# Mamba block with a 16-expert MoE: the opening in another order, router logits by four column groups

## The reference, cut to what matters

```python
# mamba
xz = xn @ W_in;  x_in, z = split(xz)               # 512 channels each
u = silu(conv4(x_in) + conv_b)                     # causal, one filter per channel
dt, B, C = split(u @ W_xproj)                      # 16, 16, 16
delta = softplus(dt @ W_dt + b_dt)
h[t] = exp(delta*A) * h[t-1] + delta*u*B           # 512 channels x 16 states
y = (sum_n h*C + D_skip*u) * silu(z);  out = y @ W_out
# moe
w, idx = top2(softmax(xn @ Wr + br))               # 16 experts, weights renormalised
h = gelu(layernorm(xn @ W1[e] + b1[e]) * g1[e] + be1[e])
moe = sum over the two experts of w * (h @ W2[e] + b2[e])
```

## Time and profile before

| | us |
|---|---|
| median of 3 runs (lowest to highest) | 1169.85 (1165.87 to 1171.04) |
| the profiled execution | 1167.6 |
| its span, first to last instruction | 1165.8 |
| VectorE busy | 1050.6 (90%) |
| TensorE / ScalarE / GpSimd busy | 956.4 / 865.6 / 842.7 |
| VectorE idle before the router chain | 10.64 |

### The profile page before, as it was taken

One profiled execution on the slowest core, in us unless ns is written; L12 is line 12 of the kernel. 1 busy time (PEld: TensorE's weight loads), 2 busy tenths in 40 slices (PEclk: granted clock), 3 DMA queues, 4 the chain that ended last, 5 costly groups with the idle time before them and its releaser, 6 DMA issues.

```text
span 1165.8 us, 16719 instructions
## 1 busy us (share of the span) xinstructions
PE 956.4 (82%) x4498; PEld 642.5 (55%) x4499; DVE 1050.6 (90%) x1308; ACT 865.6 (74%) x1793; POOL 842.7 (72%) x550
## 2 busy tenths in 40 slices
PE   5955576696978989789887998799988999978775
PEld 2433244463556656566555766476556655656554
DVE  7599969999999899989688969999898989979994
ACT  3444597655789788777799689968998699867971
POOL 8005588888668677558677786977977767867994
PEclk9975897589889999799998999899998999789978
DMA  9987865764366523834437542763447452864413
GB/s 313 405 360 231 269 197 149 250 229 106 94 220 199 120 65 95 303 103 99 104 117 258 154 102 68 266 202 62 107 140 240 130 123 58 258 195 89 107 19 64
DMA packets 130295, 194.38 MB, mean 167 GB/s; under 512 B 20892, under 2 KB 113224, under 8 KB 121944
## 3 DMA queue, kind: packets, MB, share of 16 engines
q1 hardware_dynamic: 104944, 153.06, 39.4%
q0 software_dynamic: 18816, 23.14, 12.1%
q10 hardware_dynamic: 6440, 17.10, 4.0%
HBM read 146.34 MB, written 51.05 MB: 169 GB/s over the span
## 4 chain that ended last, share of the span: by engine, by line
PE 38%; ACT 17%; issue 16%; DVE 14%; POOL 8%; DMA 6%; ACTq 2%; SPq 0%; DVEq 0%; POOLq 0%
DVE hb L1463 9%; PE psY L1020 7%; PE psA L1045 6%; POOL hc L624 5%; ACT hb L785 4%; PE psC L1157 4%; PE psC L1107 3%; PE psA L1092 3%; PE psE L1134 2%; DVE psB L1452 2%; DMA xg<-meta 2%; ACT hnT L872 2%; PE psA L1037 2%; PE psA L1080 1%; ACT L875 1%
## 5 line engine op out<-in xcount | busy, mean ns | idle before, releaser
L624 POOL TENSOR_TENSOR hc<-hb,Cb 128x1024 f32<-128x1024 f32 x235 | 595.6, 2599 | 128.7 <-PE psY L1020 69.6
L1463 DVE TENSOR_TENSOR_SCAN hb<-hb,carry,psB 128x512 f32<-128x512 f32 x384 | 471.3, 1263 | 0.8 <-ACT hb L785 0.7
L1020 PE MATMUL psY<-ident,hc 128*128 128x128 f32 x2048 | 311.7, 293 | 66.3 <-POOL hc L624 52.4
L1020 PEld LDWEIGHTS psY<-ident,hc 128*128 128x128 f32 x2048 | 261.2, 152 | 186.2 <-issue 82.8
L785 ACT ACTIVATE hb<-delta,aneg 128x512 f32<-128x512 f32 x512 | 349.2, 717 | 15.4 <-DVE delta L1301 7.0
L1452 DVE TENSOR_TENSOR psB<-Bb,psU 128x512 f32<-128x512 f32 x512 | 325.1, 679 | 0.0
L664 POOL DMA_INDIRECT out<-yo,idx x80 | 127.9, 1599 | 66.1 <-ACT yo L885 21.3
L1463 DVE TENSOR_TENSOR_SCAN hb<-hb,psB 128x512 f32<-128x512 f32 x128 | 149.2, 1201 | 4.2 <-ACT hb L785 4.2
L1045 PE MATMUL psA<-ux,dgw 128*128 128x512 f32 x232 | 119.7, 626 | 11.8 <-ACT ux L729 11.7
L638 POOL DMA_INDIRECT xs_d<-xg,slots x64 | 68.4, 1068 | 47.5 <-issue 27.1
L1157 PE MATMUL psC<-w2r,hnT 128*128 128x256 f32 x320 | 89.7, 429 | 0.0
(11 more groups left out here) (211 smaller groups left out, 1199.2 us busy)
## 6 DMA issues: line engine op xcount, KB each, us to landing
Bb<-bc_d SPq DMA_DIRECT2D x32, 1024.0 KB, 6.4
Cb<-bc_d SPq DMA_DIRECT2D x32, 1024.0 KB, 7.1
w2r<-in_L_ffn_W SPq DMA_DIRECT2D x90, 256.0 KB, 3.2
w1r<-w1c_d SPq DMA_DIRECT2D x80, 256.0 KB
xs_d<-xg ACTq DMA_DIRECT2D x1, 10320.0 KB, 41.0
xg<-xs_d SPq DMA_DIRECT2D x20, 516.0 KB, 5.2
xg<-xn_d SPq DMA_DIRECT2D x64, 128.0 KB, 2.3
Bb<-in_L_attn_x SPq DMA_DIRECT2D x8, 512.0 KB, 9.0
```

Of the source, the lines that this page charges most:

```text
L624: pool.tensor_tensor(hc[:, k:k + 2, :], hb[:, g % HR:g % HR + 2, :], Cb[:, n:n + 2, :], ALU.mult).then_inc(s_g, 1)
L1020: mm = pe.matmul(y[:, tt * P:(tt + 1) * P], hc[:, g % GR, tt * P:(tt + 1) * P], ident[:, :], start=False, stop=(n == NS - 1), is_transpose ...
L1463: dve.tensor_tensor_scan(h, h, psB[g % 2][:, :], first, ALU.mult, ALU.add).then_inc(s_scan, 1)
```

## The change

- **Router logits.** The router weights get 32 columns (16 used, the rest zero), and each group's product is four matmuls of 128 tokens per half of the inputs, written to four bands of 32 PSUM partitions. One 128x128 eviction and one 128x128 transpose follow. Logits are copied out in two halves.
- **Constants.** GpSimd writes the identity, does group 0's root, then writes the other constants, waits for W_in and conv_w, and does the diagonal matrices after groups 1 to 4. The big zero memset of VectorE moves behind the first statistics. SyncE waits for two small memsets before it loads the router weights, and loads the bias four times.
- **First projection.** Quarters 0 and 1 are projected and convolved between router groups (rounds 2 to 7), 2 and 3 after them; quarters 0 to 2 take turns in psA. The rank matmuls stand between the convolutions of quarters 2 and 3.
- **Expert table.** Its four vector instructions move from the router chain to unit 40 of chunk 0.
- **Silu.** In every chunk the last tile of z, and the last quarter of x, goes from PSUM straight through silu, after the silu of the other three; the slots of `z_silu` move from 29 to 28, from 29 to 25 in chunk 0, from 31 to 30 in the last.

The diff, cut to its core and with indentation reduced:

```diff
-X0_FROM = 4
+ETAB_AT = 40
...
-    "x_copy": [13, 25, 34, 39],
+    "x_copy": [13, 25, 34],
...
-    "z_copy": [15, 17, 26, 28],
-    "z_silu": [29],
+    "z_copy": [15, 17, 26],
+    "z_silu": [28],
...
-    "z_copy": [14, 14, 24, 25],
-    "z_silu": [29],
+    "z_copy": [14, 14, 24],
+    "z_silu": [25],
...
-    "z_copy": [13, 20, 28, 30],
-    "z_silu": [31],
+    "z_copy": [13, 20, 28],
+    "z_silu": [30],
...
-wr = sb("wr", [P, KC, E])
+wr = sb("wr", [P, KC, 2 * E])
...
-brc = sb("brc", [E, 1])
+brc = sb("brc", [P, 1])
...
-lgT = [hc[0:E, k, :] for k in range(2)]
+lgT = [hc[:, k, 0:P] for k in range(2)]
...
-    return (psA, psC, psY[0], psY[1])[dc]
+    return (psA, psA, psA, psC)[dc]
...
+        if g == 0 and h == 0:
+            sp.wait_ge(s_etab, 1)
...
-    sp.dma_start(wr[:, :, :], Wr.rearrange("(k p) e -> p k e", p=P)).then_inc(s_w["early"], 16)
-    sp.dma_start(brc[:, :], br.rearrange("(e a) -> e a", a=1)).then_inc(s_w["early"], 16)
+    sp.wait_ge(s_cdve, 2)
+    sp.dma_start(wr[:, :, 0:E], Wr.rearrange("(k p) e -> p k e", p=P)).then_inc(s_w["early"], 16)
+    for k in range(TT):
+        sp.dma_start(brc[2 * E * k:2 * E * k + E, :], br.rearrange("(e a) -> e a", a=1)).then_inc(s_w["early"], 16)
...
-    sp.wait_ge(s_cdve, 1)
...
+    pool.wait_ge(s_const, 1)
     pool.affine_select(out=ident[:, :], in_=ident[:, :], compare_op=ALU.not_equal, fill=1.0,
                        base=0, pattern=[[-1, P]], channel_multiplier=1).then_inc(s_const, 1)
...
+    def constants():
+        pool.memset(upper[:, :], 0.0).then_inc(s_const, 1)
+        pool.memset(pick6[:, :, :], 1.0).then_inc(s_const, 1)
+        pool.memset(reset, 1.0).then_inc(s_const, 1)
+        pool.wait_ge(s_const, 5)
...
+        pool.iota(iotaM[:, :], pattern=[[1, MT]], base=0, channel_multiplier=0, **kw).then_inc(s_const, 1)
...
-    pool.wait_ge(s_cdve, NCONST)
+    pool.wait_ge(s_cdve, 3)
...
-        if g == 2:
+        if g == 0:
+            constants()
             pool.wait_ge(s_w["conv"], 32)
-            pool.wait_ge(s_const, 5)
-        if 2 <= g < 2 + DC:
-            conv_weights(g - 2)
+        if 1 <= g <= DC:
+            conv_weights(g - 1)
...
-    def x_silu(p):
-        act.wait_ge(s_xe, (p + 1) * DC)
+    def x_silu(p, bank):
...
+        act.wait_ge(s_xe, (p + 1) * DC - 1)
...
+        wrap = min(first + DC - 1, UR)
+        act.activation(ux[:, first:wrap, HALO:], ux[:, first:wrap, HALO:], ACT.Silu).then_inc(s_u, 1)
+        if wrap < first + DC - 1:
+            k = first + DC - 1 - UR
+            act.activation(ux[:, 0:k, HALO:], ux[:, 0:k, HALO:], ACT.Silu).then_inc(s_u, 1)
+        act.wait_ge(s_xp, (p + 1) * DC)
+        act.activation(u_of(p, DC - 1), bank[:, :], ACT.Silu, bias=col(cb, DC - 1)).then_inc(s_xe, 1)
         act.preload_act_table_set(LNEXP)
...
     def z_silu(c):
-        act.wait_ge(s_zc, (c + 1) * TT)
-        act.activation(zs[:, :, :], zs[:, :, :], ACT.Silu).then_inc(s_z, 1)
+        act.wait_ge(s_zc, (c + 1) * TT - 1)
+        act.activation(zs[:, 0:TT - 1, :], zs[:, 0:TT - 1, :], ACT.Silu).then_inc(s_z, 1)
+        z_free(c, TT - 1)
+        act.activation(zs[:, TT - 1, :], psA[:, :], ACT.Silu).then_inc(s_zc, 1)
         act.preload_act_table_set(LNEXP)
...
+    def logits(h):
+        act.wait_ge(s_lv, (h + 1) * NC // 2)
+        half = TILES // 2
+        act.activation(lg[:, h * half * E:(h + 1) * half * E].rearrange("p (i e) -> p i e", e=E),
+                       psE[:, :].rearrange("p (i w) -> p i w", w=2 * E)[:, :, 0:E], ACT.Copy).then_inc(s_lg, 1)
...
+        if g == NC // 2 + 2:
+            logits(0)
...
-            act.activation(lgT[(g - 1) % 2], (psC, psU)[(g - 1) % 2][0:E, :], ACT.Identity, bias=brc[:, :]).then_inc(s_lc, 1)
+            act.activation(lgT[(g - 1) % 2], (psC, psU)[(g - 1) % 2][:, 0:P], ACT.Identity, bias=brc[:, :]).then_inc(s_lc, 1)
...
-        if g == X0_FROM + 2:
-            x_in(0, 0, bank0(0))
+        if g in (3, 6):
+            x_in(0, g // 3 - 1, psA)
+        if g == 5:
+            x_copy(0, 0)
...
-    act.wait_ge(s_lv, NC)
-    act.activation(lg, psE[:, :], ACT.Copy).then_inc(s_lg, 1)
-    for dc in range(1, DC):
+    x_copy(0, 1)
+    logits(1)
+    for dc in range(2, DC):
...
-    act.wait_ge(s_vec, 1)
-    for dc in range(DC):
-        act.wait_ge(s_xp, dc + 1)
-        act.activation(u_of(0, dc), bank0(dc)[:, :], ACT.Silu, bias=col(cb, dc)).then_inc(s_xe, 1)
-    act.preload_act_table_set(LNEXP)
+    x_copy(0, 2)
+    x_silu(0, bank0(DC - 1))
...
-            pe.wait_ge(s_u, p)
+            pe.wait_ge(s_u, silus(p))
+            pe.wait_ge(s_xe, (p + 1) * DC)
...
-        pe.wait_ge(s_xe, dc + 1)
         if dc == 0:
-            pe.wait_ge(s_lg, 1)
+            pe.wait_ge(s_lg, 2)
+        elif dc == DC - 1:
+            pe.wait_ge(s_xe, DC)
...
-    pe.wait_ge(s_const, 15)
-    pe.wait_ge(s_cdve, NCONST)
-    pe.wait_ge(s_w["early"], 32)
+    pe.wait_ge(s_const, 2)
...
+            if g == 1:
+                pe.wait_ge(s_w["early"], 16 * (1 + TT))
...
             for kc in range(KC):
-                mm = pe.matmul((psC, psU)[(g - 1) % 2][0:E, :], wr[:, kc, :], xnTg[g - 1][:, kc, :],
-                               start=(kc == 0), stop=(kc == KC - 1))
+                for tt in range(TT):
+                    mm = pe.matmul((psC, psU)[(g - 1) % 2][2 * E * tt:2 * E * (tt + 1), 0:P], wr[:, kc, :],
+                                   xnTg[g - 1][:, kc, tt * P:(tt + 1) * P], start=(kc == 0), stop=(kc == KC - 1))
             mm.then_inc(s_lm, 1)
         if g >= 2:
             pe.wait_ge(s_lc, g - 1)
-            for tt in range(TT):
-                i = (g - 2) * TT + tt
-                mm = pe.matmul(psE[:, i * E:(i + 1) * E], lgT[g % 2][:, tt * P:(tt + 1) * P], ident[0:E, 0:E],
-                               start=True, stop=True, is_transpose=True)
-            mm.then_inc(s_lv, 1)
...
-        if g == X0_FROM:
-            pe.wait_ge(s_w["conv"], 32)
-            pe.wait_ge(s_vec, 1)
-        if X0_FROM <= g < X0_FROM + KC:
-            project(0, 0, g - X0_FROM, bank0(0))
-        elif g == NC - 1:
-            pe.wait_ge(s_wc, DC * KW)
-            for k in range(KW):
-                convolve(0, 0, k, bank0(0))
-    pe.wait_ge(s_te, 2 * NC)
-    for dc in range(1, DC):
-        if dc == 1:
-            pe.wait_ge(s_lc, NC)
+            if g == NC // 2 + 2:
+                pe.wait_ge(s_lg, 1)
+            i = (g - 2) % (NC // 2)
+            pe.matmul(psE[:, i * P:(i + 1) * P], lgT[g % 2], ident[:, :],
+                      start=True, stop=True, is_transpose=True).then_inc(s_lv, 1)
+        if g in (2, 5):
+            if g == 2:
+                pe.wait_ge(s_w["conv"], 32)
+                pe.wait_ge(s_vec, 1)
+            else:
+                pe.wait_ge(s_xe, 1)
+            for kc in range(KC):
+                project(0, g // 3, kc, psA)
+        elif g in (3, 4, 6, 7):
+            dc = (g - 3) // 3
+            pe.wait_ge(s_wc, (dc + 1) * KW)
+            for k in range(KW // 2):
+                convolve(0, dc, g % 3 * 2 + k, psA)
...
+    pe.wait_ge(s_lc, NC)
+    for dc in range(2, DC):
+        if dc == 2:
+            pe.wait_ge(s_xe, 2)
         for kc in range(KC):
             project(0, dc, kc, bank0(dc))
-    for dc in range(1, DC):
+    pe.wait_ge(s_wc, DC * KW)
+    for dc in range(2, DC):
         for k in range(KW):
             convolve(0, dc, k, bank0(dc))
-    pe.wait_ge(s_w["big"], 16 * NBIG)
-    for dc in range(DC):
-        if dc == 0:
+        if dc == 2:
+            pe.wait_ge(s_const, 15)
+            pe.wait_ge(s_cdve, NCONST)
+            pe.wait_ge(s_te, 2 * NC)
             pe.wait_ge(s_rtd, 2)
             pe.matmul(psB[0][:, :], upper[:, :], Mb, start=True, stop=True).then_inc(s_rank, 1)
             pe.matmul(psB[1][:, :], onesb[:, :], Mb, start=True, stop=True).then_inc(s_rank, 1)
+    pe.wait_ge(s_w["big"], 16 * NBIG)
+    pe.wait_ge(s_u, silus(0))
+    for dc in range(DC):
...
-    dve.memset(zero, 0.0).then_inc(s_cdve, 1)
+    dve.memset(wr[:, :, :], 0.0).then_inc(s_cdve, 1)
+    dve.memset(brc[:, :], 0.0).then_inc(s_cdve, 1)
+    dve.memset(mhalf[:, :], -0.5).then_inc(s_cdve, 1)
...
     row_stats(0)
+    dve.memset(zero, 0.0).then_inc(s_cdve, 1)
     row_norm(0)
...
-    over = zs[:, 0:3, :].rearrange("p a b -> p (a b)")
-    cmp_t = over[:, 0:MT * E].rearrange("p (j e) -> p j e", e=E)
-    link(dve.tensor_tensor(cmp_t, s16(9).unsqueeze(1).to_broadcast([P, MT, E]),
-                           iotaT.rearrange("p (j e) -> p j e", e=E), ALU.is_le))
-    tf = over[:, MT * E:MT * E + MT]
-    link(dve.tensor_reduce(tf, cmp_t, AX.X, ALU.add))
-    link(dve.tensor_scalar(tf, tf, float(E - 1), None, ALU.min))
-    link(dve.tensor_copy(etab[:, :], tf))
+    link(dve.tensor_copy(tiles_to[:, :], s16(9)))
     dve.memset(small[:, 0, 0:1], 0.0).then_inc(s_route, 1)
     d_max(0, 0)
+    def tile_experts():
+        room = yo[:, :, :].rearrange("p a b -> p (a b)")
```

(30 more changed lines are left out.)

51 lines of the change are left out of this document (24 added, 27 removed).

## The result

The changed kernel took 1176.41 us (median of 8 runs; 1173.92 to 1186.44), the kernel before 1169.24 in runs on the same chip: ratio 1.0072, 95% interval 1.0042 to 1.0102. (One of the 8 runs of the kernel before took 1283.49 us, far above all others, and is not in the ratio.) It is **slower by 0.7%**; forecast was 1160.6 and faster, with a range up to 1176. The profiled execution took 1173.99 us (span 1172.3) against 1167.6.

What follows compares the result with a forecast made beforehand. VectorE, busy 90% of the span, was taken as the bound. Savings of 2.0 (router chain), 3.0 (chunk 0) and 4.2 us (other chunks) sum to -9.2: 1158.4 profiled, 1160.6 as median, range near 1149 to near 1176.

Steps and rivals of the forecast that it cites:

- Part 1: The start, up to router group 2: TensorE begins it at 19.6 in place of 19.46 us, +0.1.
- Part 2: TensorE from group 2 to the logits: terms sum to +1.2 us, logits at about 49.1.
- four abreast: Rival, router products: four bands run at once, logits at 45.5, total 1157 us; chance 0.18.
- drain at each change of shape: Rival, TensorE: alternating array shapes drain it, 2.6 us more, total 1163.2; chance 0.10.
- Part 3: Router chain, logits to delta: 25.8 us instead of 29.1, delta at 74.9 against 76.97, 2.0 less.
- The cover of B: Before unit 0's product: B lands at about 74.5, three us before the product at 77.8.
- About 3 us after L752: Load of B before unit 0: issued that long after source line L752, then taking 4.4 us.
- Part 4: Chunk 0 near unit 30: silu of z ends about 8 us sooner, table hidden; 3.0 us less.
- Part 5: Three other long silu waits, later chunks: each 1.4 us shorter, 4.2 less together.
- the price as nothing: Part 5, chunks 0 to 6: TensorE stands 2.3 us for psA, costed at nothing because VectorE is idle then.
- psA held too long: Rival, slot 28: TensorE waits 2.3 to 2.5 us in seven chunks, 17 us, total 1182; chance 0.14.
- the case with half of psA passed on: Variant of the psA rival: half its delay reaches the total, 1173 us; the rival's whole chance is 0.14.

Runs made afterwards that it cites:

- the run with the eleven products: Changed kernel plus eleven identity products in TensorE's idle time behind groups 0 and 1, three DMA issues put ahead of the first projection: 1175.94 us, 1.0043.
- experiment 5: Kernel before with only the router product by four column groups and what that needs: 1171.90 us, 0.9993.
- the copy at 68: Residual copy of x to out issued at unit 68 instead of 12; on the changed kernel 1174.12 us, 1.0034.
- Moving the one constant: Kernel before with `INIT_AT`, the unit issuing the residual copy of x to out, set from 12 to 68: 1165.19 us, 0.9944.

## Why the prediction was wrong, step by step

- **Part 1.** Group 2 on TensorE at 19.97 (19.6 forecast): nearly right, by luck. It took its transposes at half pace, and the constants slowed VectorE's first normalisation by 1.5 us. Both costed at nothing.
- **Part 2.** The sum was +1.2, measured +2.6 (50.46 for 49.1). A router product took 0.58 us from its start to the next record, not 1.0 (-2.9 over seven); "four abreast" was the nearer case. The half pace until 27.3 cost 3.6, as the run with the eleven products shows. That term was missing. The rest of the difference, 0.7, I can't assign. Of a drain at each change of shape the rows show nothing: product and transpose back follow each other without a gap, 28.77 + 0.65 against 29.35.
- **Part 3.** Right: from logits to delta 25.7 us (25.8 forecast), delta at 76.12. The cover of B did not hold: forecast to land at about 74.5, it was only issued at 74.39, and the first product waited 0.2 for it. "About 3 us after L752" was 5.8, as the write of B and C landed behind the zeroing of the token buffer. And the 2.0 us at delta counted whole in the sum: unit 0 did come 0.9 us sooner, and nothing of it was left at unit 16.
- **Part 4.** Units 32 to 48 took 2.8 us less (3.0 forecast), and the silu wait of chunk 0 vanished. The agreement is luck: the silus alone take 5.0 off there, more than the 3.5 that GpSimd was to allow, and the table behind unit 40 is not hidden; alone it costs its own 3.9 us there.
- **Part 5.** The three other silu waits shrank by 1.2 to 1.4 (1.4 forecast). **The step that failed is "the price as nothing"**, which I had called the weakest: the rival *psA held too long* was right in place, in price (1.4 to 2.4 us, seven times, 14 to 17 in all) and in mechanism. 4.1 to 7.7 us were passed on between units 272 and 432: not the 17, but near the half. That is as much as the 4.2 that part 5 took for its gain, so the silus alone came to 0 (1.0001).
- **The step that was missing** is what unit 0 triggers. I treated a microsecond at delta as a microsecond of the kernel. Two things do not move with unit 0: B, C and the rows, bound by DMA engines that the zeroing keeps full, and GpSimd's puts behind them. And one moves with it that should not: the residual copy. No rival named that copy. In experiment 5, 2.9 of the 6.8 us of gain went by unit 16, and the lead of 3.9 became a lag of 3.9 by unit 32, where the put waits behind the copy.
- **The chances** did not follow from the cases. By the same 0.5% the case with half of psA passed on (1173) is no change, so slower had 0.07, not 0.15.

The parts measured alone, with the copy at unit 12, are columns -0.1%, table +0.35%, silus 0, late clock about +0.3%: together +0.6%, against 0.7% measured. The intervals are each 0.2 to 0.3% wide on a side, so this sum is consistent, not proof. It leaves out the new order of the constants and of the first projection, which no run has alone, and it takes the table from one side: taken out of the changed kernel, the table's move is worth 0.1%, within the noise.

Open: why the changed opening reaches full clock early in some runs; a step of 4 us between units 256 and 272 that columns alone and the table put back show (with the copy at 68 too), and the kernel before does not; and what makes up the third of the changed kernel's 0.9% with the copy at 68 that z's silu (0.3 to 0.5%) and the clock (0.27%, within the noise) leave; I would put it to the table but did not measure it there.

## What to carry to other kernels

Before a prologue is shortened, list what in the main loop is tied to the loop's count and what to a transfer: the gain lasts only if both move, and a bulk DMA placed by unit number moves into whatever was safe before. Moving the one constant was worth more (0.56%) than the whole rebuilt opening; with column groups and x's silu it gave 0.94%, though the step from 0.56 to 0.94 is within the intervals. A shared PSUM bank held 2 us longer by one engine is not free because another engine is idle just then; ask what the bank's next user has queued behind it.
